# The gate stage of a one-core block: rounding the next weights one eviction earlier on ScalarE

## What is computed

```python
x = x + xattn(layernorm(x), ctx, ctx, 0, mask)      # 16 x 64 rows of 1024
# feed-forward, rows = 1024, hidden I = 2752
s = silu(einsum('bsh,ih->bsi', layernorm(x), w_gate))
_, idx = top_k(-abs(s), I // 2)
s = s with the entries idx of each row set to 0
s = s * einsum('bsh,ih->bsi', layernorm(x), w_up)
x = x + einsum('bsi,hi->bsh', s, w_down)
x = x + mixture(layernorm(x), router_w, router_b, A, Bm)
```

## Time and profile before

| | us |
|---|---|
| median of three runs | 1432.91 (1432.13 to 1434.08) |
| the profiled execution | 1432.05 |
| its span, first to last instruction | 1430.4 |
| TensorE busy in it | 1376.7 (96%) |
| VectorE, GpSimd, ScalarE busy | 979.0, 940.9, 729.1 |
| mean granted TensorE clock | 0.995 of 2.4 GHz |

### The profile page before, as it was taken

One profiled execution on the slowest core, in us unless ns is written; L12 is line 12 of the kernel. 1 busy time (PEld: TensorE's weight loads), 2 busy tenths in 40 slices (PEclk: granted clock), 3 DMA queues, 4 the chain that ended last, 5 costly groups with the idle time before them and its releaser, 6 DMA issues.

```text
span 1430.4 us, 30636 instructions
## 1 busy us (share of the span) xinstructions
PE 1376.7 (96%) x12775; PEld 1016.2 (71%) x12775; DVE 979.0 (68%) x1346; ACT 729.1 (51%) x920; POOL 940.9 (66%) x615
## 2 busy tenths in 40 slices
PE   3899999999999999899999999999999999999995
PEld 3555555555555555599999997888886888887873
DVE  7788888888888888880002898989794223255654
ACT  1688888888888888842325615252421111111211
POOL 0589888888888888823443352433224899999790
PEclk9999999999999999999999999999999999999998
DMA  9022323233333231023438347483727876865460
GB/s 351 2 94 94 133 94 108 94 111 105 124 107 113 96 117 53 17 75 138 159 119 312 130 169 250 166 270 119 263 91 246 291 249 197 271 189 178 152 213 32
DMA packets 111458, 217.92 MB, mean 152 GB/s; under 512 B 8320, under 2 KB 84176, under 8 KB 106320
## 3 DMA queue, kind: packets, MB, share of 16 engines
q1 hardware_dynamic: 90208, 193.34, 39.5%
q10 hardware_dynamic: 21104, 22.55, 5.1%
HBM read 173.66 MB, written 42.21 MB: 151 GB/s over the span
## 4 chain that ended last, share of the span: by engine, by line
PE 90%; DVE 5%; ACT 2%; issue 1%; POOL 0%; DMA 0%; DVEq 0%; SPq 0%; ACTq 0%
PE fast_psum L1860 17%; PE fast_psum L1752 16%; PE fast_psum L1890 16%; PE fast_psum L1770 14%; PE fast_psum L1837 14%; PE fast_psum L1789 6%; PE fast_psum L1874 1%; PE fast_psum L1796 1%; PE fast_psum L1920 1%; PE fast_psum L1941 1%; PE fast_psum L1775 1%; DVE fast_ln_stats L98 1%; ACT fast_below L1611 1%; ACT fast_g_hi L1583 1%; DVE fast_db L1325 0%
## 5 line engine op out<-in xcount | busy, mean ns | idle before, releaser
L1240 DVE TENSOR_TENSOR fast_masked<-fast_psum,fast_mask_t 128x1024 f32<-128x1024 f32 (+1 forms) x416 | 488.1, 1218 | 69.3 <-PE fast_psum L1752 67.6
L1128 POOL TENSOR_TENSOR fast_pair<-fast_probs 128x1024 f32<-128x1024 f32 x192 | 456.8, 2382 | 108.7 <-ACT fast_probs L1529 49.5
L1529 ACT ACTIVATE fast_probs<-fast_masked 128x1024 f32<-128x1024 f32 (+1 forms) x416 | 437.4, 1058 | 65.5 <-DVE fast_masked L1240 50.6
L1752 PE MATMUL fast_psum<-fast_qT,fast_kraw 32*128 32x256 f32 (+1 forms) x3328 | 247.8, 404 | 1.5 <-DVE fast_masked L1240 0.8
L1770 PE MATMUL fast_psum<-fast_probs,fast_vraw 128*32 128x256 f32 (+1 forms) x3328 | 226.5, 386 | 0.8 <-ACT fast_probs L1529 0.8
L1752 PEld LDWEIGHTS fast_psum<-fast_qT,fast_kraw 32*128 32x128 f32 (+1 forms) x3328 | 154.4, 182 | 88.7 <-DVE fast_masked L1240 54.9
L1183 POOL TENSOR_TENSOR fast_d_lo<-fast_d_raw,fast_d_hi 128x256 fp32r<-128x256 f32 (+1 forms) x264 | 199.1, 783 | 5.3
L1159 POOL TENSOR_TENSOR fast_g_lo<-fast_g_raw,fast_g_hi 128x2752 fp32r<-128x2752 f32 x14 | 86.1, 6152 | 143.0 <-ACT fast_g_hi L1583 120.9
L1837 PE MATMUL fast_psum<-fast_g_hi,fast_z_hi 128*128 128x344 f32 x512 | 164.7, 322 | 2.0 <-POOL fast_g_lo L1159 2.0
L1837 PE MATMUL fast_psum<-fast_g_lo,fast_z_hi 128*128 128x344 f32 x512 | 163.5, 319 | 0.0
L1837 PE MATMUL fast_psum<-fast_g_hi,fast_z_lo 128*128 128x344 f32 x512 | 163.3, 319 | 0.0
(11 more groups left out here) (147 smaller groups left out, 1894.3 us busy)
## 6 DMA issues: line engine op xcount, KB each, us to landing
fast_d_raw<-w_down SPq DMA_DIRECT2D x63, 512.0 KB, 3.7
fast_kraw<-ctx_t SPq DMA_DIRECT2D x32, 800.5 KB, 5.8
fast_vraw<-ctx_nat SPq DMA_DIRECT2D x16, 1536.0 KB
fast_g_raw<-w_gate SPq DMA_DIRECT2D x15, 1376.0 KB, 7.1
s<-fast_res SPq DMA_DIRECT2D x16, 688.0 KB, 3.9
fast_mag<-s SPq DMA_DIRECT2D x8, 1376.0 KB, 9.6
fast_sx<-s SPq DMA_DIRECT2D x8, 1376.0 KB, 6.9
sk<-fast_sx SPq DMA_DIRECT2D x8, 1376.0 KB, 7.2
```

Of the source, the lines that this page charges most:

```text
L1128: pool.tensor_tensor(pair[:, n % PAIR_BUFS], both[:, :, 0, :], both[:, :, 1, :], ALU.add).then_inc(paired, 1)
L1240: dve.tensor_tensor(into, of, m, ALU.add).then_inc(mask_added, 1)
L1529: act.activation(probs[0:r, g % RING, hp * HALF:(hp + 1) * HALF], masked[0:r, h % SLOTS, :], ACT.Exp).then_inc(exp_done, 1)
L1752: last = pe.matmul(scores[0:r, (2 * g + hp) % SLOTS, h % 2, i * 256:(i + 1) * 256], kraw[b % BUFS][q, u, c * P:c * P + r], qT[q, b, u, :], ...
```

## The change

In ScalarE's loop over the slots of the gate, the rounding of the weights of load n (n from 2 to 14) moves from behind the eviction of slot 4n to behind the eviction of slot 4n - 1. Within that pass of the loop it still stands ahead of a sum or a count listed at the same slot: slot 51 has a sum (tile 2), and no other slot 4n - 1 with a rounding has one. Nothing else is edited.

```diff
             for q in range(HT, SLOTS_G):
                 take_gate(q)
-                if q % HT == 0 and 2 <= q // HT < LOADS:
-                    take_weights(q // HT)
+                if (q + 1) % HT == 0 and 2 <= (q + 1) // HT < LOADS:
+                    take_weights((q + 1) // HT)
                 if q in GATE_ABS_AT:
                     measure(GATE_ABS_AT[q])
                 if q in GATE_COUNT_AT:
```

## The result

| | before | changed |
|---|---|---|
| median of 20 runs, us | 1432.91 | 1430.93 |
| the profiled execution, us (span) | 1432.05 (1430.4) | 1431.81 (1430.2) |

The ratio of the times is 0.9984, with a 95% interval of 0.9977 to 0.9991: 2.3 us less, between 1.3 and 3.3. That lies inside 0.2% and was forecast at 2.5. One execution of the changed kernel took 2264.92 us at a mean granted clock of 0.565 and isn't in the ratio.

The account below looks back on a forecast made before the run. TensorE bounds 90% of the 1430.4 us span, so only its two gate waits for low parts of weights pay: -1.40 - 1.13 = -2.53 us, other terms 0. From a mean of 1432.8 that gives 1430.2 us, range 1428.0 to 1432.6.

Parts of the forecast that it names:

- Two borders: Gate, borders of passes 12/13 and 13/14: TensorE's waits for low parts of the weights vanish, 1.40 and 1.13 us gained.
- The later stages shift as a block: After the gate: the later stages are TensorE's and everything there shifts by 2.5 us.
- The steady passes: Gate, loads 2 to 9: roundings begin 3.76 us earlier, worth nothing; subtractions already ended about 2.3 us before the border.
- Load 10: Gate: ScalarE may stand for the DMA until 768.7 to 770, slot 40's eviction late by 1 to 3 us; cost 0.
- load 14: Gate: subtraction ends at 835.4, or 838.5 if a VectorE pass of 3.08 us holds GpSimd; border at 841.0, cost 0.
- VectorE is released early: Round 1, at load 11: the earlier subtraction ends VectorE's hold at 790.2; threshold 2 comes at 791.6, 3.7 us earlier.
- Rival A: Round 1: VectorE isn't released early, threshold 3 stays at 800.24, only 0.34 and 1.13 us gained; 1431.3 us, chance 9%.
- The step on load 13: Second border: rounding at 812.8, now ahead of slot 51's sum, subtraction to 821.5, border at 826.0; 1.13 us gained.
- Rival B: Load 12: its subtraction starts before VectorE's round 3 chain ends and holds it, overrunning the second border; 1430.7 us, chance 12%.
- Rival C: Gate: subtractions hold VectorE's selection and so ScalarE's later roundings; two more holds give 1438.1 us, slower; chance 6%.
- The store and loads that come nearer to the up weights: Start of up projection: a store and 1376 KB load come closer; taken as 0, at most 2.7 us.
- Rival D: Up and down stages: later waits shrink by chance or runs lie low, -3 to -5 us, 1428 to 1429.8; chance 16%.

Follow-up runs that it names:

- experiment 1: The changed kernel run again with no edit, for a second profile; 0.9989 of the time of the kernel before.
- experiment 4: Against the kernel before, only the roundings of loads 2 to 10 moved; 1.0003 of its time.
- experiment 5: Against the kernel before, all thirteen roundings moved one eviction later, behind slot 4n + 1; 1.017 of its time, 24.3 us slower.
- experiment 2: Against the kernel before, only the rounding of load 11 moved; 0.9986 of its time.
- experiment 3: Against the kernel before, all roundings moved but that of load 11; 0.9995 of its time.
- experiment 6: The changed kernel with five more 128x2 operations in VectorE's chain of round 3 of the first pair; 0.9987 of the kernel before.
- experiment 7: The changed kernel with x's loads for the first row tiles issued at step 6 of the down projection, not step 0; 0.998 of the kernel before.
- experiment 8: The kernel before, no rounding moved, with x's first loads issued at step 6 of the down projection instead of step 0; 1.0002 of its time.
- experiment 9: The changed kernel with ScalarE's copy of tile 0 for the mixture one step earlier (47, not 48); 0.9965 of the kernel before, median 1427.81 us.

## Why the prediction was right

*The place and the price.* Two borders, 1.40 and 1.13 us, 2.53 in sum: both waits are gone and four passes are 2.54 us shorter (62.70 to 60.16). The ratio's 2.3 us (1.3 to 3.3) holds it. The median of 1430.93 stands 0.7 us over the forecast of 1430.2. I had started from the mean of four times, 1432.8, so 0.1 us of that is the start; the rest is within the interval of the ratio, and a late down weight or a fall of the clock in some of the executions would be enough for it.

*The later stages shift as a block.* The up projection does (its first matmul came at 856.58 instead of 859.32), and all up to the tail does in experiment 1. In the first profile and in six others a late down weight took some of it back, which the prediction had no term for.

*The steady passes are worth nothing.* Shown by experiment 4, and that they were close to being worth something by experiment 5. The cover I read as 2.3 us measured 2.0; no term hung on it.

*Load 10 waits for its DMA.* 2.08 us, and the eviction behind it 1.1 us late, at no cost, as bounded.

*Whether a pass of VectorE holds GpSimd*, which the prediction left open at load 14: nothing stood in GpSimd's way there (it began at 828.91), but a row of the kernel before shows that it can. VectorE's pass of 3.08 us ran from 848.46 to 851.54, and this cast, which takes 1.05 us a few microseconds on, ended 0.9 us behind it:

```profile
850.10 2.34 POOL L1167 CAST fast_u_hi<-fast_u_raw 128x1024 fp32r<-128x1024 f32 x1 [8.48 <-DMA fast_u_raw<-w_up_t]
```

*VectorE is released early, and this is what opens the first border.* Threshold 2 was expected at 791.6 and came at 791.31, threshold 3 at 796.5 and came at 796.20, and the execution ran 0.2 us early in all. Rival A is out: in experiments 2, 3 and 6 the hold follows the subtraction wherever either is put. The Trainium skill (SBUF — State Buffer, section on SBUF's two separate sides) gives that as an exclusive lock kept for a whole instruction; the trace agrees, with 2.02, 3.10, 3.47 and 5.98 us for operations that take 0.16 alone, each ending with the subtraction.

*What I had not drawn from my own steps:* that this one release frees the second border too. With load 11 alone moved, the later rounds are early enough for the old places of the roundings of loads 12 and 13. The step on load 13 credits the border to its own move ahead of the sum; experiment 2 shows that it was not needed.

*Rival B* had the right mechanism and a price that was too high. The order can flip (6), but a chain held at its last operation runs on at once, and no wait follows. A hold at the first operation, for which the price was worked out, wasn't tried. *Rival C* didn't show: GpSimd's subtractions held small operations of the selection five times before (0.86, 3.47, 3.41, 3.69 and 6.17 us long) and three times in the changed kernel (2.02, 3.10 and 0.90), besides the pass at 832.23. *The store and loads that come nearer to the up weights* cost nothing; TensorE's wait at the start of the up projection stayed at 0.5 us.

*Rival D* didn't come: 1430.93 us isn't in its 1428 to 1429.8, and its 3 to 5 us meet the interval (1.3 to 3.3) in the last 0.3 us only. It was right that the later stages move from run to run. What moves them in these profiles is a late down weight (0 to 2.1 us), a fall of the clock at 1317 us (1.67 us or none) and the clock in the tail.

## What to carry to other kernels

When a wait is behind an engine's order, follow the chain back past the engine named: here TensorE waited for GpSimd, GpSimd for ScalarE, ScalarE for VectorE, and VectorE for an earlier instruction of GpSimd, so that one rounding moved by 3.8 us (it now begins at 781.22) cleared two waits some 30 and 46 us later. Move one item at a time when a change moves thirteen. And price a change of 0.2% by the stage it touches, over a distance between two fixed events (60.16 against 62.70), because the whole span of one execution carries more scatter than that.

## What the runs showed of the hardware

- A VectorE operation on 128x2 float32 values is held by a GpSimd instruction on SBUF for up to its whole length (5.98 us instead of 0.16). The waiting time is inside the shown duration. What decides isn't the size alone. Of the small operations that began inside a GpSimd instruction, over 0.35 us ahead of its end, in the twelve profiles, all `TENSOR_TENSOR` and `SCALAR_TENSOR_TENSOR` with both inputs in SBUF were held, one on 128x1 too, and so was `TENSOR_SCALAR` on 128x2 and 128x8 (3.69 us at 824.69 before). `TENSOR_SCALAR` on 128x1 ran through (0.15 us), and so did a reciprocal on 128x2, which has one input, and a `TENSOR_TENSOR` on 128x8 with one input in PSUM (0.17 us at 1326.83 before, while GpSimd was in three subtractions on end from 1325.60 to 1327.90). From experiment 7, operations with the GpSimd instruction that they began in ahead of them:

```profile
1035.62 1.04 POOL L1167 CAST fast_u_hi<-fast_u_raw 128x1024 fp32r<-128x1024 f32 x1 [5.05 <-PE fast_psum L1860]
1035.78 0.17 DVE L1330 RECIPROCAL fast_da<-fast_da 128x2 f32<-128x2 f32 x1
1035.98 0.70 DVE L1332 TENSOR_TENSOR fast_da<-fast_da,fast_db 128x2 f32<-128x2 f32 x1
...
1058.02 1.07 POOL L1167 CAST fast_u_hi<-fast_u_raw 128x1024 fp32r<-128x1024 f32 x1 [7.67 <-PE fast_psum L1860]
1058.22 0.89 DVE L1369 TENSOR_TENSOR fast_settled<-fast_found,fast_ends 128x1 f32<-128x1 f32 x1
```

- The granted clock fell to the lower level behind an idle time of TensorE of 1.9 us, in five of ten profiles with that same wait (the changed kernel and experiments 2, 3, 6 and 7); it stayed up in the other five (before and experiments 1, 4, 5 and 8). A fall cost 1.6 to 1.7 us there (from the first of the 16 matmuls to the first of the next such group it took 8.83 to 8.91 us with it and 7.22 or 7.23 without). Behind the wait of 2.1 us for a down weight it fell in experiment 7 (0.52 from 1118 to 1121 us) and not in the changed kernel (1.00), which had the same wait. No edit of the gate explains which execution falls.
- In the tail, where TensorE works in short groups, the mean granted clock over the first 8 us came out in one of three ranges, and the tail's length with it: 1.00 and 27.6 us (experiment 7), 0.79 and 28.2 to 28.7 us (before, the changed kernel, experiments 6 and 9), 0.66 to 0.72 and 29.5 to 30.1 us (the other seven). That is 2.5 us of scatter with no edit of the tail.
